# Edge counts in four groups with centred fields, row statistics on ScalarE, and a reordered graph stage

## The chip, the core and the metric

One NeuronCore of a Trainium2 chip runs the whole program. The metric is the device time of one execution in microseconds. The engines are TensorE (PE; its weight loads are PEld), VectorE (DVE), ScalarE (ACT), GpSimd (POOL) and SyncE (SP), which issues most DMAs. Each runs its own list of instructions in order; they wait for each other by semaphores.

## What is computed

625 nodes with 768 features pass through two layers, each a graph part and a mixture of experts. The change touches only the first layer's graph convolution, its attention, and the norm ahead of its experts:

```python
z = layernorm(x)                                   # 625 x 768, over the features
row, col = src, dst, each with n loops added       # 20625 edges in src, dst
dinv = rsqrt(segment_sum(1, col))                  # degrees
x = x + segment_sum((z @ W)[row] * (dinv[row] * dinv[col])[:, None], col) + b
u = layernorm(x)
xn = rmsnorm(u) * norm1_w                          # queries = keys = values, 12 heads of 64
ao = softmax(xn_h @ xn_h.T / sqrt(64)) @ xn_h      # for each head h
xf = rmsnorm(u + ao) * norm3_w                     # goes to the router, the shared and the routed experts
x = x + u + ao + moe(xf)
```

The second layer (attention over edges, then experts of width 1536) reads the same matrix of edge counts.

## The kernel before

**Edge counts.** The edges become a 625 x 625 matrix of counts CT: 165 chunks of 125 edges. For each chunk VectorE writes a one-hot of the sources (L1396, 628 columns) and one of the targets (L1397, 314 columns), in two-byte floats; the targets' 625 columns are folded to 314 by giving the upper half the weight 4096 (`FIELD`). TensorE multiplies them (L2042, L2045: 4 x 314 + 2 x 157 columns) into PSUM. A ring of five chunks (`EU`) lies between. One PSUM sum holds lower + 4096 x upper count, so the chunks are cut into six groups (`GROUPS`), which alternate between two halves of PSUM. After each group the sum is unpacked: ScalarE rounds out the upper part (`upper_counts`, L1047 to L1051), VectorE subtracts it (`lower_counts`, L1404, L1406) and adds both parts to CT (L1417, L1427). A constant row of 1 and -66 (`SHIFT`) keeps the lower part centred. VectorE does this between the next group's one-hots, along with the row statistics of x (L1366), their mean and root, and the norm (L1378). TensorE transposes the first half of the normed rows late in the last group.

**Node products and sums over edges.** All float32 products are made of two-byte pairs: high x high, low x high, high x low. Once the counts are done, ScalarE splits off their high part CTh (L1067), VectorE the low part CTl (L1473). TensorE makes h in five tiles of 125 rows (`node_products`, 36 matmuls each, L2073), the degrees as 50 matmuls of CTh and CTl with a column of ones (L2097), and transposes the counts for a mask and for layer 2 (`counts_turned`, float32, L2083). ScalarE scales h by the root into hth (L1039), VectorE makes the rest htl (L1487). The sum over edges (L2120, L2124) runs tile by tile; the self loop is a product with the identity (L2122).

**Norm of the tiles.** For each tile VectorE adds the sum to the rows (`summed`, L1503), takes their statistics (L1509, L1513) and asks ScalarE for two roots (L1080). It refines them in four small steps between the next tile's work, and ends with two scalars (L1561, L1562). ScalarE then writes the tile's 12 heads twice (L1083, L1085) and the normed row z (L1087), VectorE their low part (`heads_low`, L1527). The next root stands behind these on ScalarE.

**Heads.** For 12 heads and five tiles: TensorE transposes the heads (`sides_transposed`, L2138), makes scores (L2153, L2155), VectorE their maximum (L1579), ScalarE the exponential (L1104). TensorE transposes the weights (L2172), VectorE copies them (L1588), ScalarE makes the high part (L1113), GpSimd the low part (L961). TensorE makes the weighted sum one head behind (L2186), ScalarE takes it out (`sum_out`, L1120), TensorE turns it back (`sum_back`, L2194), VectorE divides (`fin`, L1601), GpSimd adds it to z (`head_joined`, L968). Then all engines meet (`fence`), ScalarE squares z (L1026), VectorE multiplies z by the norm's weight (L1782), the root is taken, and ScalarE scales the rows (L1168) for the shared expert.

The order is written out by hand for each engine. The program prints the functions that the diff touches:

## Time and profile before

| | us |
|---|---|
| median of 3 runs | 1620.09 (1619.05 to 1623.38) |
| profiled execution | 1621.49 |
| its span | 1619.9 |
| edge counts | to 137.8 |
| sums over edges begin | 189.1 |
| first exponential of the heads | 230.8 |
| first scaled row ahead of the experts | 393.5 |
| TensorE busy in the span | 1474.3 (91%) |
| VectorE, ScalarE, GpSimd busy | 1263.2, 873.3, 332.4 |

The span runs from the first to the last instruction; the profiled execution's own time is 1.6 us longer. A row of a timeline gives start, duration and the instruction, and in brackets how long its engine had been idle and for whom. Durations of neighbours on one engine overlap a little, so a rhythm is read from starts.

### The profile page before, as it was taken

Reading aid. Unit: us, or ns where it says so; the run is one execution under the profiler, and the core shown is the slowest. Engines: PE = TensorE matmul, PEld = TensorE weight load, DVE = VectorE, ACT = ScalarE, POOL = GpSimd, SP = SyncE. Lnnn points to the kernel's source line nnn. Section 1 sums busy time; section 2 is a strip of 40 time slices with the busy share of each in tenths; the row PEclk is TensorE's granted clock in tenths of the full one; section 3 lists DMA queues with packets and bytes.
Section 4 is the critical chain, followed back from the end, with each engine's and each line's share of the span. In section 5 each row is a group of like instructions: output and inputs, shape, how many; then the busy total and the mean of one; then the engine's idle time right before and its main releaser. Section 6 shows DMA issues by size and latency. Waiting matters only on the chain.

```text
span 1619.9 us, 36985 instructions
## 1 busy us (share of the span) xinstructions
PE 1474.3 (91%) x14673; PEld 1271.2 (78%) x14673; DVE 1263.2 (78%) x2191; ACT 873.3 (54%) x1235; POOL 332.4 (21%) x254
## 2 busy tenths in 40 slices
PE   7988968885999999999999889866999999999996
PEld 5666756664767899999998644445999999999994
DVE  8998477774565688888888679867988888888785
ACT  1113257776344567776775135554666665666651
POOL 0000416562040000000004047753600000000050
PEclk9999979997999999999999779977999999999999
DMA  7640000002475788888886011126888888888883
GB/s 203 157 121 1 11 0 1 1 1 98 138 231 174 253 276 300 302 297 296 305 286 197 1 32 32 33 88 214 280 311 285 301 285 296 302 290 295 294 267 96
DMA packets 55557, 297.61 MB, mean 184 GB/s; under 512 B 14064, under 2 KB 14320, under 8 KB 32434
## 3 DMA queue, kind: packets, MB, share of 16 engines
q1 hardware_dynamic: 41761, 263.23, 47.9%
q0 software_dynamic: 13712, 33.26, 7.6%
q8 instruction: 54, 0.88, 0.2%
q14 instruction: 30, 0.24, 0.0%
HBM read 264.07 MB, written 32.34 MB: 183 GB/s over the span
## 4 chain that ended last, share of the span: by engine, by line
PE 69%; DVE 19%; ACT 4%; issue 3%; POOL 2%; DMA 2%; SPq 0%; POOLq 0%; DVEq 0%; ACTq 0%
PE ps L744 14%; PE ps L723 9%; PE ps L725 9%; PE ps L727 9%; PE ps L2274 5%; PE ps L2257 5%; DVE wl L1396 3%; DVE wl L1397 3%; PE ps L2386 2%; POOL wl L996 2%; DMA ext<-in_units 2%; PE ps L2186 2%; DVE wl L600 2%; PE ps L756 1%; PE ps L2172 1%
## 5 line engine op out<-in xcount | busy, mean ns | idle before, releaser
L723 PE MATMUL ps<-big,wh 128*128 128x176 f16 x2160 | 496.3, 240 | 9.0 <-DVE wl L600 5.2
L727 PE MATMUL ps<-big,wl 128*128 128x176 f16 x2160 | 496.4, 238 | 0.0
L725 PE MATMUL ps<-big,wh 128*128 128x176 f16 x2160 | 496.3, 238 | 0.0
L744 PE MATMUL ps<-big,wh 128*128 128x176 f16 x2160 | 262.7, 238 | 3.8 <-DVE big L634 3.8
L744 PE MATMUL ps<-big,wl 128*128 128x176 f16 x1080 | 248.9, 239 | 0.0
L600 DVE SCALAR_TENSOR_TENSOR wl<-ext,wh 128x2304 f16<-128x2304 f32 x90 | 229.7, 2552 | 1.5 <-issue 0.9
L600 DVE SCALAR_TENSOR_TENSOR wl<-raw,wh 128x2304 f16<-128x2304 f32 x90 | 229.5, 2550 | 0.0
L519 ACT ACTIVATE wh<-raw 128x2304 f16<-128x2304 f32 x90 | 190.4, 2117 | 57.5 <-PE ps L744 53.7
L723 PEld LDWEIGHTS ps<-big,wh 128*128 128x128 f16 x2160 | 208.7, 97 | 12.8 <-issue 4.3
L519 ACT ACTIVATE wh<-ext 128x2304 f16<-128x2304 f32 x90 | 190.5, 2117 | 51.2 <-PE ps L744 35.6
L725 PEld LDWEIGHTS ps<-big,wh 128*128 128x128 f16 x2160 | 211.2, 98 | 0.2
L727 PEld LDWEIGHTS ps<-big,wl 128*128 128x128 f16 x2160 | 208.2, 96 | 0.0
L744 PEld LDWEIGHTS ps<-big,wh 128*128 128x128 f16 x2160 | 188.3, 97 | 5.3 <-DVE big L634 4.8
L2042 PE MATMUL ps<-wl 126*128 126x314 f16 x660 | 113.9, 300 | 19.5 <-DVE wl L1397 19.4
L744 PEld LDWEIGHTS ps<-big,wl 128*128 128x128 f16 x1080 | 104.4, 97 | 0.0
L961 POOL TENSOR_TENSOR ext<-raw,ext 125x625 f16<-125x625 f32 x60 | 80.3, 1339 | 103.0 <-ACT ext L1113 102.5
L486 POOL DMA_DIRECT2D y_slots<-big x16 | 11.7, 733 | 420.0 <-ACT big L549 420.0
L996 POOL TENSOR_TENSOR wl<-wl,logs 125x625 f32<-125x625 f32 x60 | 83.2, 1414 | 68.8 <-DVE wl L1935 68.8
L630 DVE TENSOR_TENSOR big<-ps,ext 128x176 f32<-128x176 f32 x108 | 36.6, 339 | 67.3 <-ACT ext L542 65.2
L2042 PEld LDWEIGHTS ps<-wl 126*128 126x128 f16 x660 | 59.7, 99 | 35.6 <-DVE wl L1397 14.7
L2386 PE MATMUL ps<-raw,wh 125*65 125x512 f32 x240 | 80.7, 481 | 6.1 <-ACT raw L1243 6.1
L480 POOL DMA_DIRECT2D big<-x_slots x17 | 12.7, 745 | 343.3 <-PE ps L707 304.7
(363 smaller groups left out, 2814.5 us busy)
## 6 DMA issues: line engine op xcount, KB each, us to landing
raw<-in_units SPq DMA_DIRECT2D x54, 1152.0 KB
ext<-in_units SPq DMA_DIRECT2D x54, 1152.0 KB
raw<-in_units SPq DMA_DIRECT2D x36, 1153.0 KB, 5.9
ext<-in_units SPq DMA_DIRECT2D x36, 1153.0 KB, 6.4
raw<-in_units_s SPq DMA_DIRECT2D x16, 769.0 KB, 4.6
ext<-in_units_s SPq DMA_DIRECT2D x16, 769.0 KB, 4.5
x_slots<-raw SPq DMA_DIRECT2D x1, 8976.0 KB
big<-x_slots POOLq DMA_DIRECT2D x17, 528.0 KB, 8.6
```

The costliest lines, as they stand in the source:

```text
L519: nc.scalar.activation(wh[:, u % RING, 0:ph.wide], raw[u % RING][:, 0:ph.wide], ACT.Copy, scale=WS).then_inc(ph.hi, 1)
L600: nc.vector.scalar_tensor_tensor(out=wl[:, u % RING, 0:ph.wide], in0=raw[u % RING][:, 0:ph.wide], scalar=WS, in1=wh[:, u % RING, 0:ph.wide ...
L723: nc.tensor.matmul(o, wh[:, u % RING, w_], x_, start=c == 0 and m == 0, stop=False, skip_group_check=True)
L725: nc.tensor.matmul(o, wh[:, u % RING, w_], xTl[:, c, 0:ph.n], start=False, stop=False, skip_group_check=True)
L727: ins = nc.tensor.matmul(o, wl[:, u % RING, w_], x_, start=False, stop=c == KC - 1, skip_group_check=True)
L744: ins = nc.tensor.matmul(o, l_[:, u % RING, w_], r_, start=first and k == 0 and c % 2 == 0, stop=last and k == 2, skip_group_check=True)
L961: nc.gpsimd.tensor_tensor(pT[:, 1, h % 2, :, own], key_blocks(n), pT[:, 0, h % 2, :, own], ALU.subtract).then_inc(s_wlo, 1)
L996: nc.gpsimd.tensor_tensor(power[:, (h * NT + t) % 4, :], power[:, (h * NT + t) % 4, :], logs[:, t, :], ALU.add).then_inc(s_masked, 1)
L2042: nc.tensor.matmul(ps[:, at + i * BANK:at + i * BANK + TH], hot[0:k, s, i * P:i * P + 128], hot[0:k, s, TP:TP + TH], start=first, stop=las ...
L2257: ins = nc.tensor.matmul(shared_up(j)[:, 0:n], l_[:, j % RING, w_], r_[:, c, t0 * P:t1 * P], start=c == 0 and k == 0, stop=c == KC - 1 and ...
L2274: ins = nc.tensor.matmul(shared_sum(t)[:, n0:n1], l_[:, j % 2, own], r_[:, j % RING, D + n0:D + n1], start=fresh and k == 0, stop=last and ...
L2386: ins = nc.tensor.matmul(sumsT[:, n0:n1], values[:, t, h, :], prob[:, t, n0:n1], start=t == 0, stop=t == NT - 1)
```

## The change

- The counts are made in four groups of 9, 8, 8 and 8 (times five chunks). The field is 5792, the constant row carries 50 and -7276 (`CENTRE`) so that both parts are centred, and `MIDDLE` is added back when unpacking. ScalarE rounds after scaling by 1/5792.
- The sources' one-hot is 626 columns wide; the two columns that were spare hold ones for all edges, so that the last row of CT's wider view CTD (127 partitions) is the degrees. Five float32 transposes (`degree_rows`) bring them to the partitions; the 50 matmuls go.
- The row statistics and the norm of x move from VectorE to ScalarE, ahead of its first unpacking: a sum, a sum of squares of the centred rows, a root, five scaled rows.
- On ScalarE the degrees' root stands ahead of the split of the counts. On VectorE the degrees and two bias rows come first, then the root, then three bias rows and the low counts.
- The self loop is no product any more: VectorE adds dinv^2 x h to the rows (second instruction of `node_low`). The counts are transposed from two-byte CTh, into two PSUM banks in turn.
- In the norm of the tiles the next root is asked before the last small step and is taken on ScalarE ahead of this tile's heads. Of tile 4 only head 0 is written before the heads begin; the other eleven and row z follow once the first sides are out.
- The squares of z are taken in four parts (`PARTS`): heads 0 to 3 during head 6, 4 to 7 during head 10, 8 to 10 behind the last exponential, head 11 after the fence. z times the weight likewise runs in two parts ahead of the fence, and head 11 is added to z by VectorE straight from PSUM.
- At the end ScalarE takes head 10's sum out ahead of the last high weights.

```diff
-GROUPS = ((0, 6), (6, 12), (12, 18), (18, 23), (23, 28), (28, 33))
+GROUPS = ((0, 9), (9, 17), (17, 25), (25, 33))
 TP, TH, TQ = 628, 314, 157
-FIELD = 4096.0
-SHIFT = 66.0
-ROUND = 1.5 * 2.0 ** 35
+PD, ROWS = P + 2, 626
+FIELD = 5792
+CENTRE = (50, 7276)
+ROUND = 1.5 * 2.0 ** 23
+MIDDLE = tuple(divmod(CENTRE[0] * CENTRE[1] * EU * (j1 - j0), FIELD) for j0, j1 in GROUPS)
...
+PARTS = (0, 4 * HD, 8 * HD, 11 * HD, D)
...
+            def squares(g, t):
+
+                own = slice(PARTS[g], PARTS[g + 1])
+                nc.scalar.activation(junk[t][:, own], z[:, t, own], ACT.Square,
+                                     accum_out=st[:, t, g, 0:1]).then_inc(s_part, 1)
...
+            act.wait_ge(s_x, 32)
+            for t in range(NT):
+                nc.scalar.activation(z[:, t, :], xres[:, t, :], ACT.Identity,
+                                     accum_out=st[:, t, 0, 0:1]).then_inc(s_part, 1)
+            act.wait_ge(s_part, NT)
+            nc.scalar.activation(st[:, :, 1, 0], st[:, :, 0, 0], ACT.Copy, scale=-1.0 / D).then_inc(s_part, 1)
+            act.wait_ge(s_part, NT + 1)
+            for t in range(NT):
+                nc.scalar.activation(z[:, t, :], xres[:, t, :], ACT.Square, bias=st[:, t, 1, 0:1],
+                                     accum_out=st[:, t, 2, 0:1]).then_inc(s_part, 1)
+            root()
+            count["sq"] += 1
+            act.wait_ge(s_var, count["sq"])
+            for t in range(NT):
+                nc.scalar.activation(z[:, t, :], xres[:, t, :], ACT.Identity, bias=rs[:, 2, t:t + 1],
+                                     scale=rs[:, 3, t:t + 1]).then_inc(s_rowsok, 1)
             upper_counts(0)
-            root()
...
-            act.wait_ge(s_unp, 3 * len(GROUPS))
+            root()
             nc.scalar.activation(CTh, CT, ACT.Copy).then_inc(s_nh, 1)
-            root()
...
+            both_roots(0)
+            for t in range(NT):
+                if t + 1 < NT:
+                    both_roots(t + 1)
                 count["sq"] += 1
                 act.wait_ge(s_var, count["sq"])
-                nc.scalar.activation(vst[t][:, :, 0, :], all_heads(t), ACT.Copy,
-                                     scale=pair[:, 2, t, 1:2]).then_inc(s_vh, 1)
-                nc.scalar.activation(vst[t][:, :, 2, :], all_heads(t), ACT.Copy,
-                                     scale=pair[:, 2, t, 1:2]).then_inc(s_vh, 1)
-                nc.scalar.activation(z[:, t, :], xres[:, t, :], ACT.Identity, bias=pair[:, 2, t, 0:1],
-                                     scale=pair[:, 3, t, 0:1])
+                if t + 1 < NT:
+                    heads_high(t, 0, H)
+                    row_out(t)
+            heads_high(NT - 1, 0, 1)
...
+            heads_high(NT - 1, 1, H)
+            row_out(NT - 1)
...
+                if h in (6, 10):
+                    if t == 0:
+                        act.wait_ge(s_madd, h - 2)
+                    squares((h - 6) // 4, t)
+            sum_out(H - 2)
             weight_high(H * NT - 1)
-            sum_out(H - 2)
+            act.wait_ge(s_madd, H - 1)
+            for t in range(NT):
+                squares(2, t)
...
-                nc.vector.tensor_scalar(hot[0:P, s, 0:TP], iota16[:, :], edges_f[:, 0, c:c + 1], None, ALU.is_equal)
+                nc.vector.tensor_scalar(hot[0:P, s, 0:ROWS], iota16[:, 0:ROWS], edges_f[:, 0, c:c + 1], None, ALU.is_equal)
...
+            dve.wait_ge(s_deg, 1)
+            nc.vector.tensor_scalar(rs[:, 0, :], degree_rows()[:, :, PD - 1], 1.0, None, ALU.add).then_inc(s_var, 1)
+            dve.wait_ge(s_vec[0], 16)
+            dve.wait_ge(s_vec[1], 16)
+            for t in range(2):
+                nc.vector.tensor_tensor(xres[:, t, :], xres[:, t, :], vec[:, 0, :], ALU.add)
+            root_of(dinv[:, :])
+            step(nc.vector.tensor_scalar(rs[:, 3, :], dinv[:, :], 1.0 / WS, None, ALU.mult))
+            step(nc.vector.tensor_tensor(rs[:, 2, :], rs[:, 3, :], dinv[:, :], ALU.mult))
+            nc.vector.memset(dot[0:1, 0:1], 0.0).then_inc(s_var, 1)
+            for t in range(2, NT):
+                ins = nc.vector.tensor_tensor(xres[:, t, :], xres[:, t, :], vec[:, 0, :], ALU.add)
...
+                nc.vector.scalar_tensor_tensor(out=xres[:, t, :], in0=node_sum(t), scalar=rs[:, 2, t:t + 1],
+                                               in1=xres[:, t, :], op0=ALU.mult, op1=ALU.add).then_inc(s_aggv, 1)
...
+            node_low(0)
+            node_low(1)
+            masked_counts(0)
+            masked_counts(1)
+            node_low(2)
+            masked_counts(2)
+            masked_counts(3)
+            node_low(3)
+            masked_counts(4)
+            node_low(4)
...
+                if more_:
+                    both_roots_asked(t + 1)
                 step(nc.vector.tensor_tensor(inv, inv, tmp, ALU.mult))
...
-                    both_roots_asked(t + 1)
-                heads_low(t)
+                    row_weighted_1(t + 1)
+                    dve.wait_ge(s_vh, 2 * t + 1)
+                    heads_low(t, 0, H)
+            dve.wait_ge(s_vh, 2 * NT - 1)
+            heads_low(NT - 1, 0, 1)
...
+            dve.wait_ge(s_vec[0], 32)
+            dve.wait_ge(s_madd, H - 1)
+            row_weighted(0, PARTS[3])
+            dve.wait_ge(s_mback, H)
+            for t in range(NT):
+                ins = nc.vector.scalar_tensor_tensor(
+                    out=z[:, t, PARTS[3]:D], in0=bank(7)[0:P, 128 + t * HD:128 + (t + 1) * HD],
+                    scalar=cols[:, 4 + (H - 1) % 2, t:t + 1], in1=z[:, t, PARTS[3]:D], op0=ALU.mult, op1=ALU.add)
+            ins.then_inc(s_madd, 1)
+            dve.wait_ge(s_madd, H)
+            step(row_weighted(PARTS[3], D))
...
+            for n0, n1 in ((0, BANK), (BANK, D)):
+                node_products(0, n0, n1)
+            node_products(1, 0, BANK)
+            pe.wait_ge(s_unp, 3 * len(GROUPS))
+            for i in range(NT):
+                ins = nc.tensor.transpose(degree_rows()[:, i, 0:PD], CTD[:, NT - 1, i * P:(i + 1) * P],
+                                          ident[0:PD, 0:PD])
+            ins.then_inc(s_deg, 1)
+            node_products(1, BANK, D)
+            for t in range(2, NT):
+                if t >= 3:
+                    pe.wait_ge(s_aggv, t - 2)
                 node_products(t, 0, BANK)
+                if t == 2:
+                    pe.wait_ge(s_var, 3)
+                    pe.wait_ge(s_nh, NH_CT + 1)
+                counts_turned(2 * t - 4)
                 node_products(t, BANK, D)
+                if t < 4:
+                    counts_turned(2 * t - 3)
...
-                        nc.tensor.matmul(o, ident16[0:P, 0:P], r_[:, i, n0:n1], start=False, stop=False)
```

The order of TensorE after the last edge chunk, before (from the 256-column half of row tile 0 on; `raw` and `big` hold W's high part and the rows, `wl` the split counts, L2097 are the degrees, L2083 transposed counts):

```order
L2073 MATMUL ps<-raw,big 125x256 x18
L2073 MATMUL ps<-raw,big 125x512 x18
L2073 MATMUL ps<-raw,big 125x256 x18
L2097 MATMUL ps<-iota,wl 125x1 [waits s_node_low]
L2097 MATMUL ps<-iota,wl 125x1 x49
L2083 MATMUL ps<-ident,big 125x125 [waits s_var]
L2083 MATMUL ps<-ident,big 125x125 x4
L2073 MATMUL ps<-raw,big 125x512 x18
L2073 MATMUL ps<-raw,big 125x256 x18
L2083 MATMUL ps<-ident,big 125x125 [waits s_cdv]
L2083 MATMUL ps<-ident,big 125x125 x4
L2073 MATMUL ps<-raw,big 125x512 [waits s_node_low]
```

And after (L2153 are the node matmuls, L2175 the degrees, L2163 transposed counts):

```order
L2153 MATMUL ps<-raw,big 125x256 x18
L2153 MATMUL ps<-raw,big 125x512 x18
L2175 MATMUL ps<-ident,big 125x127 [waits s_unp]
L2175 MATMUL ps<-ident,big 125x127 x4
L2153 MATMUL ps<-raw,big 125x256 x18
L2153 MATMUL ps<-raw,big 125x512 x18
L2163 MATMUL ps<-ident,wl 125x125 [waits s_node_high,s_var]
L2163 MATMUL ps<-ident,wl 125x125 x4
L2153 MATMUL ps<-raw,big 125x256 x18
L2163 MATMUL ps<-ident,wl 125x125 x5
L2153 MATMUL ps<-raw,big 125x512 [waits s_aggv]
L2153 MATMUL ps<-raw,big 125x512 x17
```

The degrees stand ahead of tile 1's second half, need only CT itself, and are five transposes; tile 3 waits for VectorE's self term (`s_aggv`) and no longer for the low part of h.

VectorE at the same place, before (L1359 ends the gate's split, L1473 makes the low counts, L1477 adds the bias rows, L1479 reads the degrees, L1487 the low part of h, L1493 a mask):

```order
L1359 SCALAR_TENSOR_TENSOR g<-gates,g 128x6x8 [waits s_v]
L1473 TENSOR_TENSOR wl<-big,wl 125x3125 [waits s_node_high,s_v]
L1477 TENSOR_TENSOR xres<-xres,vec 125x768 [waits s_vec1,s_vec0]
L1477 TENSOR_TENSOR xres<-xres,vec 125x768 x4
L1479 TENSOR_SCALAR rs<-ps 125x5 [waits s_deg]
L1330 RECIPROCAL dinv<-rs 125x5 [waits s_sq]
L1331 TENSOR_TENSOR rs<-dinv 125x5 [waits s_v]
L1332 TENSOR_TENSOR rs<-rs 125x5 [waits s_v]
```

And after (L1518 degrees, L1522 and L1528 bias rows, L1530 low counts):

```order
L1518 TENSOR_SCALAR rs<-ps 125x5 [waits s_deg,s_v]
L1522 TENSOR_TENSOR xres<-xres,vec 125x768 [waits s_vec1,s_vec0]
L1522 TENSOR_TENSOR xres<-xres,vec 125x768
...
L1526 MEMSET dot 1x1 [waits s_v]
L1528 TENSOR_TENSOR xres<-xres,vec 125x768 x3
L1530 TENSOR_TENSOR wl<-big,wl 125x3125 [waits s_node_high]
L1536 SCALAR_TENSOR_TENSOR xf<-ps,rs,xf 125x768 [waits s_node_high,s_v]
L1538 SCALAR_TENSOR_TENSOR xres<-ps,rs,xres 125x768
L1536 SCALAR_TENSOR_TENSOR xf<-ps,rs,xf 125x768 [waits s_node_high]
L1538 SCALAR_TENSOR_TENSOR xres<-ps,rs,xres 125x768
```

The low counts have moved behind degrees, root and bias rows, and each low part of h is followed by the self term.

ScalarE in the norm of the tiles, before (L1080 roots, L1083 and L1085 heads, L1087 row z):

```order
L1080 ACT_TABLE_LOAD [waits s_var]
L1080 ACTIVATE pair<-pair 125x2 [waits s_logs]
L1083 ACTIVATE wh<-ext,pair 125x12x64 [waits s_var]
L1085 ACTIVATE wh<-ext,pair 125x12x64
L1087 ACTIVATE z<-xres,pair 125x768
L1080 ACTIVATE pair<-pair 125x2 [waits s_var]
L1083 ACTIVATE wh<-ext,pair 125x12x64 [waits s_var]
```

And after (L1107 roots, L1112 heads, L1117 row z):

```order
L1107 ACT_TABLE_LOAD [waits s_var]
L1107 ACTIVATE pair<-pair 125x2 [waits s_logs]
L1107 ACTIVATE pair<-pair 125x2 [waits s_var]
L1112 ACTIVATE wh<-ext,pair 125x12x64 [waits s_var]
L1112 ACTIVATE wh<-ext,pair 125x12x64
L1117 ACTIVATE z<-xres,pair 125x768
L1107 ACTIVATE pair<-pair 125x2 [waits s_var]
L1112 ACTIVATE wh<-ext,pair 125x12x64 [waits s_var]
```

The roots of tile t + 1 stand ahead of the heads of tile t.

## Rows read from the trace of the kernel before

**Rows 1.** Windows, all engines: stretch, length, busy us (x instructions), PEclk, DMA share, GB/s.

```profile
10.00:50.00 40.00, 37.94 (x320) 28.75 (x319) 38.62 (x123) 5.83 (x6) 0.00 (x0) 1.00 0.73 204
...
222.00:226.00 4.00, 0.29 (x1) 0.10 (x1) 2.01 (x9) 2.72 (x5) 0.00 (x0) 0.50 0.00 0
260.00:280.00 20.00, 18.32 (x144) 13.48 (x140) 14.75 (x30) 14.58 (x29) 12.74 (x10) 1.00 0.00 1
```

**Rows 2.** Waits of 0 to 140 us: us in total, times, longest.

```profile
PE ps L2042 <- DVE wl L1397: 19.4, 15, 7.9
```

**Rows 3.** Timeline, VectorE: start, duration, instruction.

```profile
60.76 0.37 DVE L1396 TENSOR_SCALAR wl<-iota,edges_f 125x628 f16<-125x628 f16 x1
...
63.02 0.37 DVE L1396 TENSOR_SCALAR wl<-iota,edges_f 125x628 f16<-125x628 f16 x1
```

**Rows 4.** Timeline, TensorE, edge chunks.

```profile
9.15 1.25 PE L2042 MATMUL ps<-wl 126*128 126x314 f16 x4
...
50.20 0.71 PE L2042 MATMUL ps<-wl 126*128 126x314 f16 x4
...
57.61 0.69 PE L2042 MATMUL ps<-wl 126*128 126x314 f16 x4
```

**Rows 5.** Groups by line of 0 to 330 us: busy, mean ns | idle before.

```profile
L1396 DVE TENSOR_SCALAR wl<-iota,edges_f 125x628 f16<-125x628 f16 x165 | 61.6, 373 | 1.5 <-PE ps L2045 1.1
...
L1404 DVE SCALAR_TENSOR_TENSOR wl<-wh,ps 125x1256 f32<-125x1256 f32 x6 | 8.7, 1452 | 2.3 <-ACT wh L1051 2.3
...
L1417 DVE TENSOR_TENSOR big<-big,wh 125x1560 f32<-125x1560 f32 x5 | 8.9, 1771 | 0.0
...
L1366 DVE BATCH_NORM_STATS2 st<-xres 125x6 f32<-125x384 f32 x10 | 5.0, 542 | 0.0
...
L1378 DVE TENSOR_SCALAR z<-xres,mv,rs 125x768 f32<-125x768 f32 x5 | 3.3, 663 | 0.0
```

**Rows 6.** Timeline, graph stage: ScalarE, VectorE, then TensorE.

```profile
137.84 1.22 ACT L1047 ACTIVATE wh<-ps 125x1256 f32<-125x1256 f32 x1 [5.58 <-PE ps L2045]
...
156.63 3.42 DVE L1473 TENSOR_TENSOR wl<-big,wl 125x3125 f16<-125x3125 f32 x1 [1.83 <-ACT wl L1067]
...
150.22 8.25 PE L2073 MATMUL ps<-raw,big 128*125 128x512 f16 x55 [0.44 <-DVE raw L1461]
160.10 3.17 PE L2097 MATMUL ps<-iota,wl 125*125 125x1 f16 x50 [1.63 <-DVE wl L1473]
...
165.72 7.99 PE L2073 MATMUL ps<-raw,big 128*125 128x512 f16 x36
...
174.09 6.02 PE L2073 MATMUL ps<-raw,big 128*125 128x512 f16 x36
...
189.10 1.29 PE L2120 MATMUL ps<-xf,wl 125*125 125x512 f16 x5 [1.50 <-DVE xf L1487]
```

**Rows 7.** Timeline, tiles' norm and first head: VectorE, TensorE, ScalarE.

```profile
206.15 0.17 DVE L1541 RECIPROCAL pair<-pair 125x2 f32<-125x2 f32 x1 [0.81 <-ACT pair L1080]
...
211.96 0.17 DVE L1541 RECIPROCAL pair<-pair 125x2 f32<-125x2 f32 x1 [0.82 <-ACT pair L1080]
...
222.82 0.29 PE L2138 MATMUL ps<-ident,wh 125*128 125x125 f16 x1 [5.58 <-DVE wh L1527]
...
228.51 1.28 ACT L1104 ACT_TABLE_LOAD   x1
230.80 0.78 ACT L1104 ACTIVATE raw<-ps,cols 125x625 f32<-125x625 f32 x1 [1.01 <-DVE cols L1579]
```

**Rows 8.** Timeline, end of the heads: TensorE, then ScalarE.

```profile
378.31 3.76 PE L2186 MATMUL ps<-ext,wh 125*128 125x512 f16 x16 [0.63 <-issue]
...
386.53 0.84 ACT L1026 ACTIVATE big<-z 125x768 f32<-125x768 f32 x1 [3.19 <-DVE rs L1346]
...
390.79 1.28 ACT L1019 ACT_TABLE_LOAD   x1
...
393.46 1.76 ACT L1168 ACTIVATE xf<-xf,rs 125x768 f32<-125x768 f32 x2 [1.17 <-DVE dot L1785]
```

183 lines of the change are left out of this document (79 added, 104 removed).

## The prediction

> **What bounds the kernel now.** I read the page's slices and the chain first, then the windows, the waits, the groups by line and the timelines of the four places that the diff touches. All lie before 395 us of a span of 1619.9 us; behind them the diff only renames, so everything later should move as a block. Up to about 137 us the edge counts run. VectorE is busy 38.62 of 40 us there and TensorE 37.94 [rows 1], which looks like a tie; but TensorE stood still 15 times for a one-hot, 19.4 us in all, 7.9 of them at the start: 11.5 us belong to VectorE [rows 2]. In the attention heads all engines take turns and TensorE is the fullest (18.32 of 20 us) [rows 1].
>
> **Edge counts.** One chunk costs VectorE (63.02 - 60.76) / 4 = 0.565 us [rows 3] and TensorE (57.61 - 50.20) / 11 = 0.674 us, once its clock is up [rows 4]. So TensorE is the slower of the two, and only VectorE's other work makes it wait. Removed from VectorE: ten half-row statistics (10 x 0.542 = 5.4 us), five norms (5 x 0.663 = 3.3), about 0.6 of means, and two of five unpackings inside the loop, each 1.452 + 0.39 for the low part and two additions of 1.771, less overlap 5.14 us, so 10.3 [rows 5]. Together 19.6. Left on VectorE from 7.3 us on: 165 x 0.565 = 93.2, a first unpacking of 4.0, two of 5.14, a root of 1.3: end 116. TensorE's floor is the new bound: start at 8.1, four chunks at the low clock (1.31 us each, from the four matmuls of 1.25 against 0.71 later [rows 4]), 161 x 0.674 = 108.5, 15 transposes between of 1.75: 123.6. To this come waits. The ring holds five chunks. An unpacking gives pauses of 1.76, 1.69 and 1.69 us, five chunks apart, and five chunks win back only 5 x 0.109 = 0.55; a full ring (3.4 us less the handing over) is empty at the third pause, about 1 us short. Following both engines chunk by chunk with these numbers I get 137.9 for the present kernel (the trace has 137.84 [rows 6]) and 126.6 for the new one, 3.0 of it waits. **-11.2 us**; bounds: -14.3 with no wait at all, -8 if the waits double.
>
> ScalarE's new work there is hidden. Five rows summed and five squared at 0.84 us (the duration of a square of 768 columns [rows 8]), two table loads of 1.28, five norms of 0.92. x is on chip somewhere between 11 and 17.7 us, so the squares end at 22 to 28; VectorE asks for the root only after 35 chunks, at about 31. The norms end near 40.3, and group 0 (45 chunks now) at 40.9: ScalarE is free 0.6 us before it must unpack. If it is late, the unpacking slips behind ring slack; price at most 1 us.
>
> The one-hot row shrinks from 628 to 626 columns, which is no multiple of four. L1396 takes 373 ns for 628 columns [rows 5]; a slower element rate would hit 165 instructions. The Trainium skill (Vector Engine (DVE) Microarchitecture Reference, section 5.1) says that the four-element rate needs two-byte operands and an even or matching outermost count, and that an uneven last tick only drops its missing element; by that rule nothing changes. No row of this case shows 626 columns; the rival below prices it.
>
> **Graph stage**, counted from E, the end of the counts (137.8 now). Unchanged up to E+17, where VectorE has finished the low weights, both additions and the gates. Now: TensorE runs until 158.5 (55 matmuls from 150.22), VectorE splits the counts (3.42 us, from 156.63), and 50 one-column matmuls for the degrees take 3.17 [rows 6]; that slow patch also costs the clock: behind it the 36 matmuls of row tile 2 take 7.99 us against 6.02 for tile 3 [rows 6]. New: after 54 of the 72 node matmuls, E+18.4, five transposes of 0.14 us bring the degrees at E+19.1. VectorE adds two bias rows (1.8), takes the root (1.0) and two factors: E+22.6. ScalarE, which now does the root ahead of the split, ends the high counts at E+22.5 and the first two high node tiles at E+24.4. VectorE is late next: three bias rows (2.7), low counts (3.4), then low tile and self term, 0.95 each. The first self term ends at E+30.6; TensorE has finished tiles 0 to 2 and two transposed counts by E+27.6 and waits 3.0 us for that PSUM bank. Tiles 3 and 4 take 5.8 each plus 0.4 per transposed count: E+43.5. High part, low part 2.0: the sums over edges start at E+45.6, against 189.10 = E+51.3 [rows 6]. **-5.7 us.**
>
> Then 20 identity matmuls go, 2 x (0.215 + 0.110) us per tile; TensorE needs 4.9 instead of 5.5 per tile (0.65 less). The rhythm now is 211.96 - 206.15 = 5.81 us [rows 7] and belongs to a loop: ScalarE does the heads and the row before the next root, so VectorE stands 0.8 us at the reciprocal. With the root asked and taken ahead of the heads, VectorE's own work is left: 4.93 us from reciprocal to the end of the low heads, plus 0.14 for the high heads, 5.07. Walked through: first sum out E+50.5; second tile E+55.4; then 60.5, 65.6, 70.6; last root E+76.5; one head of tile 4 and not twelve: transposes ready E+78.0, sides out E+78.9. Now the sides are out at 228.5 = E+90.7, where the table load before the first exponential begins [rows 7]. From the start of the sums that is 33.3 against 39.4: **-6.1 us.** The eleven heads and the row left over (0.85 + 0.85 + 0.92) now stand on ScalarE between the sides and the first exponential, with its table load behind them: E+82.75 against 230.80 = E+93.0 [rows 7]: **+1.5 us** given back. Bounds of these three together: -14 to -5.
>
> TensorE's clock: in the wait of 3.0 us it may fall. In the present kernel it fell within a gap of 5.58 us that ended at 222.82 [rows 7]: it stands at 0.50 in 222 to 226 us [rows 1]. The new gap is little over half of that one, and matmuls fill the time before it. I take no fall; a fall costs what tile 2 shows, 7.99 - 6.02 = 2.0 us, plus 0.6 of transposes. The Trainium skill (TensorE: Matmul & The Clock Gate, "Part 4: PE-mode transpose") says transposes do not count as activity of the array as matmuls do; the five ahead of the gap would then lengthen it, and the sum be 2.6 us worse. The trace's slow patch behind one-column matmuls is akin but does not decide it.
>
> **Heads.** Ten squares of 256 columns join ScalarE in heads 6 and 10. A square of 768 takes 0.84 [rows 8]; by columns plus the fixed part 0.42 each. ScalarE is busy 14.58 of 20 us [rows 1]; four of five squares fall in its idle, the one at tile 4 delays an exponential that TensorE takes up at once, by 0.34. **+0.7 us**, bounds 0 and 10 x 0.42 = 4.2.
>
> **End of the heads.** The last weighted sum starts at 378.31 [rows 8], waiting for head 10's sum and the low weights on GpSimd. ScalarE now takes head 10 out 1.5 us sooner, then GpSimd (two tiles until 377.3) ends last: -0.9. Behind the last sum_back at 384.7 now stand a join on GpSimd (0.9), squares from 386.53 (5 x 0.84), a table load at 390.79, the root and the first scaled row at 393.46 [rows 8]: 8.8 us. New: five small PSUM additions 0.8, five 64-column products 0.7, fence 0.2, five squares of 64 columns 1.6, table load 1.28, root 1.3: 5.9. The product over 704 columns and squares of 192 run beside the last weighted sum. 0.9 + 2.9 = **-3.7 us** rounded; bounds -6 (the slow clock there, 16 matmuls in 3.76 us, gone too) and -2.
>
> **Sum.** -11.2 - 5.7 - 6.1 + 1.5 + 0.7 - 3.7 = -24.5. The profiled execution took 1621.49 us (1.6 around its span), so 1597.0; the median of the runs is 1.4 lower: 1595.6, told as 1596.
>
> **Rivals.**
> (a) The clock falls in the new wait and VectorE's waits are dearer: edge -8, graph stage 2.6 worse, squares 2 worse: 1603.6. For it: every one of these stretches hands over between engines, and I let nearly all latencies vanish. 0.16.
> (b) Deeper gain: the gap before the heads shrinks from 5.6 us [rows 7] to under 4 and the heads start at full clock. Now the first ten microseconds of heads run at half clock; five tiles with scores and transposes slower by about 0.8 each, so 4 us, and 1.6 at the tail: 1590. Against: I count 4.9 us of gap. 0.10.
> (c) Shown no gain in the edge stage: the change does not do what it says, because ScalarE's statistics come late (x late) or TensorE's ring waits stay 11.5 us; then only the later parts count, -13.3: 1607. Against it rows 2 to 4. 0.05.
> (d) The slower side: the 626-column one-hot loses its element rate. Half rate adds 628 x 0.26 = 0.163 us per chunk; VectorE at 0.73 then bounds the stage, E = 145, which still leaves 1614. At a quarter of the rate it adds 0.49: VectorE needs 165 x 1.055 = 174 plus 16, E = 197, and the total is 1621 + 59 - 13 = 1667. It decides from 0.21 us more per one-hot: the counts may end at 126.6 + 24.5 = 151 before all is lost, and VectorE ends at 116 + 165 x 0.21. Against: 314 columns, also no multiple of four, cost 0.275 from issue to issue. 0.03.
>
> **How the numbers follow.** Forecast 0.66, (a) 0.16, (b) 0.10, (c) 0.05, (d) 0.03. The forecast's own range is 1591 to 1601. To hold 8 in 10 I take in (b) and (a) and stop short of (c): 1588 to 1605. What a measurement of this kernel can tell from no change is 0.3%, 4.9 us. Only (d) ends slower: faster 0.96, same 0.01, slower 0.03.
>
> **What would show it.** Counts end near 126.6 us; TensorE's waits for one-hots fall from 19.4 to about 11; edge sums start 45.6 us behind that; rhythm of the tiles 5.1; first exponential near 209; a stand of TensorE near 3 us before tile 3, clock at 1.00 after it; first scaled row 5.9 us behind the last sum_back. Wrong if the one-hot's duration moves from 373 ns, if VectorE waits for ScalarE's roots in the loop, or if an exponential in heads 6 and 10 is late at every tile.

## The result, and the profile after

The changed kernel took 1604.58 us (median of 4 executions, 1600.18 to 1608.05), beside 1621.37 us for the kernel before on the same chip: a ratio of 0.9892, 95% interval [0.9872, 0.9912], so 17 us less, a gain 7 to 8 us smaller than forecast. Another set of five executions, made during the experiments, gave 1598.63 (1598.10 to 1601.08) beside 1620.75: 0.9859 [0.9836, 0.9882], a gain of 22. So the gain is 17 to 22 us, depending on the set. The predicted 25 lies outside the interval of the first (14 to 21) and inside that of the second (19 to 27).

The profiled execution took 1604.37 us (span 1602.6). In the windows (columns as in [rows 1]) TensorE is now the fuller engine in the counts, 40.00 of 40 us against VectorE's 37.70, and its clock falls behind the counts and at row tile 3, where in the kernel before it fell only behind the one-column matmuls (tile 2 of [rows 6]); at the start of the heads it is low as before (0.53; 0.55 in 219 to 237 us of the kernel before):

```profile
10.00:50.00 40.00, 40.00 (x342) 31.04 (x341) 37.70 (x121) 19.68 (x32) 0.00 (x0) 1.00 0.73 202
126.00:142.00 16.00, 11.51 (x46) 7.14 (x45) 11.89 (x15) 5.92 (x8) 0.00 (x0) 0.68 0.00 0
158.00:166.00 8.00, 6.15 (x26) 3.78 (x27) 6.32 (x9) 0.72 (x1) 7.04 (x1) 0.79 0.00 0
204.00:222.00 18.00, 8.93 (x39) 6.30 (x39) 10.67 (x31) 11.43 (x19) 1.29 (x1) 0.53 0.00 0
```

The waits of 0 to 130 us. TensorE's waits for one-hots fell from 19.4 us in 15 times [rows 2] to

```profile
PE ps L2122 <- DVE wl L1452: 10.9, 6, 8.1
```

as forecast (about 11). ScalarE shows a wait that the prediction does not have at all:

```profile
ACT raw L1088 <- DMA y_slots<-raw: 19.4, 1, 19.4
```

The one-hot's groups (45 to 115 us; busy, mean ns | idle before): 626 columns take 380 ns, against 373 for 628 in [rows 5].

```profile
L1451 DVE TENSOR_SCALAR wl<-iota,edges_f 125x626 f16<-125x626 f16 x95 | 36.1, 380 | 0.4
```

The graph stage (start, duration, instruction), ScalarE, VectorE, then TensorE, answers to [rows 6]:

```profile
120.77 4.51 ACT L1088 ACTIVATE raw<-ext 128x768 f16<-128x768 f32 x6 [19.43 <-DMA y_slots<-raw]
125.18 1.83 ACT L1044 ACTIVATE big<-ps 128x625 f16<-128x625 f32 x3
127.38 1.22 ACT L1058 ACTIVATE wh<-ps 127x1256 f32<-127x1256 f32 x1 [0.36 <-PE ps L2125]
...
127.05 2.25 DVE L1400 TENSOR_TENSOR big<-ps,big 128x625 f16<-128x625 f32 x3 [2.38 <-ACT big L1044]
...
129.35 2.94 PE L2113 MATMUL ps<-ident,z 125*128 125x125 f32 x15 [2.01 <-DVE big L1400]
134.28 6.99 PE L2153 MATMUL ps<-raw,big 128*125 128x512 f16 x17 [1.99 <-issue]
...
147.83 0.71 PE L2175 MATMUL ps<-ident,big 127*125 127x127 f32 x5
...
159.85 5.79 PE L2153 MATMUL ps<-raw,big 128*125 128x512 f16 x18 [2.91 <-DVE xres L1538]
...
168.01 4.05 PE L2153 MATMUL ps<-raw,big 128*125 128x512 f16 x18
...
176.41 3.30 PE L2198 MATMUL ps<-xf,wl 125*125 125x512 f16 x10 [2.09 <-DVE xf L1536]
179.51 2.02 PE L2201 MATMUL ps<-xf,wl 125*125 125x512 f16 x5
```

ScalarE begins the high split of the node weights (L1088) only when the zero fill of y_slots has landed, at 120.77. So the high rows of the first half (L1044) end at 127.0; VectorE's low rows (L1400) and the second transposes on TensorE (L2113) come late, and these transposes start 2.0 us behind the counts, run at half clock (2.94 us; 1.82 in e11_after_again at full clock), and so do the first node matmuls (17 in 6.99 us). Row tile 3, behind its wait of 2.91 us, takes 5.79 us for 18 matmuls where tile 4 takes 4.05. The degrees' transposes (L2175) start 20.4 us behind the counts and not 18.4 as forecast, and the first sums over edges are slow again.

The tiles' norm and the first head (VectorE, TensorE, ScalarE) answer to [rows 7]: the rhythm of the reciprocals is 5.02 us, not 5.81, and none of them waits (the first tile's, at 187.37, still did: 0.68). TensorE still stands 4.79 us for the last but one tile's heads. The first exponential starts at 215.54, not 230.80.

```profile
203.09 0.16 DVE L1602 RECIPROCAL pair<-pair 125x2 f32<-125x2 f32 x1
...
208.11 0.16 DVE L1602 RECIPROCAL pair<-pair 125x2 f32<-125x2 f32 x1
...
208.25 0.28 PE L2218 MATMUL ps<-ident,wh 125*128 125x125 f16 x1 [4.79 <-DVE wh L1587]
...
211.09 0.69 ACT L1135 ACTIVATE big<-ps 128x625 f16<-128x625 f16 x1 [1.16 <-PE ps L2218]
...
214.25 1.28 ACT L1145 ACT_TABLE_LOAD   x1
215.54 0.78 ACT L1145 ACTIVATE raw<-ps,cols 125x625 f32<-125x625 f32 x1
```

The end of the heads (TensorE, then ScalarE) answers to [rows 8]:

```profile
362.23 3.82 PE L2266 MATMUL ps<-ext,wh 125*128 125x512 f16 x16 [1.50 <-POOL ext L975]
...
366.63 0.69 ACT L1161 ACTIVATE big<-ps 128x625 f32<-128x625 f32 x1 [1.85 <-PE ps L2266]
...
374.64 1.76 ACT L1218 ACTIVATE xf<-xf,rs 125x768 f32<-125x768 f32 x2 [1.17 <-DVE dot L1865]
```

Measured between anchors in the profiled executions, in us (E is the start of the last ScalarE unpacking):

```
                            before   forecast   after   zeros from xf (e1_zero)
E                           137.84    126.6    127.38   126.66
E to sums over edges         51.26     45.6     49.03    45.40
sums to first exponential    41.70     37.15    39.13    39.12
to head 11's sum taken out  151.85    151.65   151.09   150.85
to first scaled row          10.81      7.9      8.01     8.01
first scaled row at         393.46    369.0    374.64   370.04
from there to the end      1226.44   1226.44  1227.96  1228.16
```

### The profile page after: what moved, and what is told of

Its sections match the earlier page's. It is cut to its first block, busy times and chain, and to the rows that moved or that the text cites. A ratio compares the mean times of both kernels' runs of the same rounds, so it can differ in the third digit from the quotient of the medians.

```text
span 1602.6 us, 36904 instructions
## 1 busy us (share of the span) xinstructions
PE 1472.8 (92%) x14608; PEld 1271.1 (79%) x14608; DVE 1253.8 (78%) x2181; ACT 883.2 (55%) x1287; POOL 332.0 (21%) x253
## 4 chain that ended last, share of the span: by engine, by line
PE 67%; DVE 16%; ACT 4%; POOL 4%; DMA 3%; issue 3%; another core or an unknown queue 1%; SPq 0%; DVEq 0%; ACTq 0%; POOLq 0%
PE ps L758 13%; PE ps L737 9%; PE ps L739 9%; PE ps L741 9%; PE ps L2354 5%; PE ps L2337 5%; POOL wl L1009 2%; DMA ext<-in_units 2%; DVE wl L1451 2%; PE ps L2266 2%; PE ps L2466 2%; DVE wl L1452 2%; DVE wl L614 2%; PE ps L770 1%
```

## The experiments

Three explanations stand against each other. Theory Z: what is missing in the graph stage is the zero fill. Theory K: the rest is TensorE's clock, which falls in waits that the forecast took as harmless. Rival P: the engines' own chain is late there. E stays the start of the last unpacking on ScalarE. Unless said otherwise, times inside a kernel are those of its one profiled execution.

**e1_zero**: the zeros come from another tile, and ScalarE waits for the fill only ahead of its first write to that tile, behind the counts.

```diff
-            nc.gpsimd.memset(raw01[:, 0, 0:D], 0.0).then_inc(s_const, 1)
+            nc.gpsimd.memset(xf[:, 0, :], 0.0).then_inc(s_const, 1)
-                         raw01[0:B // 2, 0:1, 0:D].to_broadcast([B // 2, 2 * NTAB + 2, D])).then_inc(s_zero, 16)
+                         xf[0:B // 2, 0:1, :].to_broadcast([B // 2, 2 * NTAB + 2, D])).then_inc(s_zero, 16)
...
-            act.wait_ge(s_zero, 48)
             act.wait_ge(s_wg, 16)
...
+            act.wait_ge(s_zero, 48)
             node_high(0)
```

> The changed kernel, but the zeros that are written to x_slots and y_slots now come from xf and not from raw01, so the high split of the node weights (which overwrites raw01) no longer waits for that fill (19.4 us of wait on ScalarE in the changed kernel, ending at 120.8 us). Theory Z (the fill is what made the graph stage start late): the weight split runs well before 120 us, VectorE goes on to the low rows at once (no 2.4 us wait behind its last one-hot), the second batch of transposes starts within 1 us of the end of the counts (2.0 before), everything behind is 2 to 3 us earlier, and if the shorter gap also keeps TensorE's clock at 1.00 there, up to 5: 1604.6 falls to 1600 (1599 to 1602.5). Rival P (VectorE's and TensorE's own chain was late anyway): at most 1 us, 1603.6 to 1605.

Measured: 1599.81 us (1596.47 to 1602.16), ratio to before 0.9856 [0.9834, 0.9879]. Timeline, ScalarE then TensorE:

```profile
100.54 4.49 ACT L1087 ACTIVATE raw<-ext 128x768 f16<-128x768 f32 x6
...
126.47 1.76 PE L2113 MATMUL ps<-ident,z 125*128 125x125 f32 x15
...
157.18 4.10 PE L2153 MATMUL ps<-raw,big 128*125 128x512 f16 x18 [2.91 <-DVE xres L1538]
...
172.06 3.77 PE L2198 MATMUL ps<-xf,wl 125*125 125x512 f16 x10 [2.09 <-DVE xf L1536]
175.63 1.54 PE L2201 MATMUL ps<-xf,wl 125*125 125x512 f16 x5
```

The weight split runs at 100.54, the second transposes follow the counts without a wait, and the sums start 45.40 us behind E: the forecast had 45.6. Theory Z holds for that execution of the changed kernel, and P falls. Of the 3.6 us, 2.0 had been lost by the start of tile 3 (E + 32.5 there, E + 30.5 here), 1.1 of them by the second transposes at half clock (2.94 us for 1.8). The other 1.7 came through the clock in tile 3 itself: behind the same wait of 2.91 us it takes 4.10 us here and not 5.79. That this second part belongs to the fill is not shown; e8_norm_order and e11_after_again speak against it.

**e2_fill_graph** keeps TensorE busy in the two waits:

```diff
+            def fill(n):
+                for _ in range(n):
+                    nc.tensor.matmul(bank(7)[0:P, 384:512], ident16[0:P, 0:P], iota16[0:P, 0:128], start=True, stop=True)
...
+                if t == 2:
+                    fill(40)
                 if t < 4:
                     counts_turned(2 * t - 3)
+            pe.wait_ge(s_cdv, 4)
+            fill(30)
             pe.wait_ge(s_nl, NL_CT + 1)
```

> As e1_zero, and TensorE runs 40 matmuls of 128 columns with no use in its wait ahead of row tile 3 of the node products, and 30 in its wait ahead of the sums over edges, so that it never stands still there. Theory K (the clock falls because TensorE stood still): granted clock 1.00 through tile 3 and through the first sums; the 18 matmuls of 512 columns of tile 3 take 4.05 us and not 5.79, the first 15 of the sums 3.6 and not 5.3; against e1_zero -3 us (-2 to -4). Rival: the filling delays what it stands ahead of, or the clock falls all the same: 0 to +1.5 against e1_zero.

Measured: 1596.32 us (1594.99 to 1604.93), 0.9841 [0.9820, 0.9863]. TensorE's timeline:

```profile
154.54 2.50 PE L2112 MATMUL ps<-iota,ident 125*125 125x128 f16 x40
...
157.90 4.10 PE L2159 MATMUL ps<-raw,big 128*125 128x512 f16 x18 [0.58 <-DVE xres L1538]
...
170.53 1.91 PE L2112 MATMUL ps<-iota,ident 125*125 125x128 f16 x30
172.78 2.34 PE L2208 MATMUL ps<-xf,wl 125*125 125x512 f16 x10 [0.34 <-DVE xf L1536]
174.97 1.24 PE L2211 MATMUL ps<-xf,wl 125*125 125x512 f16 x5
```

The first 15 matmuls of the sums take 3.4 us, against 5.1 in e1_zero (3.77 + 1.54, less their overlap), and the first exponential comes 37.36 us behind the sums' start, not 39.12: 1.8 us from the clock alone. That is the distance forecast (37.15). The filling delays nothing. Tile 3 gained nothing, since its clock had held in e1_zero too. So the expected 3 us were 1.8. The medians of the two lie 3.5 us apart, more than these anchors explain.

**e3_fill_heads** adds fill(76), fill(20) and fill(30) ahead of the sides of tiles 3 and 4 and of the third scores.

> As e2_fill_graph, and the same filling in TensorE's waits ahead of the heads: 76 matmuls ahead of the side of row tile 3, 20 ahead of tile 4, 30 ahead of the third scores. Theory K: the clock stays at 1.00 from 205 to 222 us, where it is 0.50 in the changed kernel; the first heads' scores and transposes take 0.38 and 0.77 us from the start and not 0.65 and 1.37: against e2_fill_graph -3.5 us (-2 to -5; my estimate of 4 for the start of the heads in the prediction's rival b). Rival: ScalarE (five exponentials of 0.78 and their partners) sets the pace there and TensorE's low clock is hidden: 0 to -1.

Measured: 1596.40 us (1592.33 to 1598.76), 0.9842 [0.9821, 0.9864]. Its window at the start of the heads, where the changed kernel has 0.53 (204 to 222 above):

```profile
200.00:218.00 18.00, 13.34 (x133) 10.68 (x132) 11.66 (x27) 14.17 (x25) 3.71 (x3) 1.00 0.00 1
```

The first head takes 9.95 us from exponential to exponential, against 11.65; to head 11's sum taken out it is 147.88 us against 149.53 in e2_fill_graph. So the slow clock at the start of the heads costs 1.7 us: not the 3.5 expected here, nor the 4 of rival (b). ScalarE, busy 14.17 of the 18 us, may set part of the pace there; no run separates that. The medians of e2_fill_graph and e3_fill_heads do not show the 1.7 us.

**e5_stats** puts the rows' statistics and norms back on VectorE, with the old row_stats, row_means and row_normed; four groups stay.

```diff
-                    if j == 6:
-                        row_roots_asked()
-                    if j == 7:
-                        rows_shifted()
+                    if 2 <= j <= 6:
+                        ins = row_stats(j - 2)
+                    if j == 10:
+                        row_means()
+                    if j == 12:
+                        root_of(rs[:, 3, :])
+                    if j in (16, 17, 18, 22, 23):
+                        ins = row_normed((16, 17, 18, 22, 23).index(j))
```

> The changed kernel with one part undone: the statistics, means and norms of the rows ahead of the counts are VectorE's again (ten half rows, five aggregates, five norms), four groups kept. My prediction's sum: VectorE has 9.3 us more to do; five norms come back at full, statistics at the start find TensorE at its low clock. By following the two engines: TensorE bounds the stage, so of 9.3 us some 5 come back (counts end at 132, 131 to 134), 1604.6 + 5 = 1609.5 (1608 to 1612). Rival Z: with the zero fill landing at 120.7 the stage behind the counts was late anyway, so that 2 of these 5 us cost nothing: 1607.5.

Measured: 1603.89 us (1597.65 to 1607.27), 0.9889 [0.9870, 0.9909]. ScalarE:

```profile
122.18 4.51 ACT L1073 ACTIVATE raw<-ext 128x768 f16<-128x768 f32 x6 [17.47 <-DMA y_slots<-raw]
126.59 1.83 ACT L1044 ACTIVATE big<-ps 128x625 f16<-128x625 f32 x3
130.74 1.22 ACT L1058 ACTIVATE wh<-ps 127x1256 f32<-127x1256 f32 x1 [2.32 <-PE ps L2128]
```

The time lies below both that were expected (1609.5 and 1607.5). E is 130.74, only 3.4 later than in the changed kernel, where 5 were expected. And the sums start at 176.15 against 176.41: nothing lost against that execution. The fill lands at 122.18 here, 8.6 us ahead of E, and delays nothing (the degrees' transposes start at E + 18.5, tile 3 takes 4.10 us); there the fill cost 2.0 us and the clock in tile 3 another 1.7. Against e11_after_again, the second execution of the changed kernel, where the sums start at 174.31, undoing the move costs 1.8 us.

**e6_zero_stats** is e5_stats with the zeros from xf.

> e1_zero (zeros from xf) with the rows' statistics and norms back on VectorE, as in e5_stats. Theory Z (the fill that lands at 120.7 us binds only a count stage that ends before about 130): counts end at 130.7 as in e5_stats and the sums over edges start 45.4 us behind them, at 176.1, so this is e5_stats over again (1603.9) and 4 us slower than e1_zero. With e5_stats and the changed kernel apart by nothing that makes the statistics' move worth 4 us alone and 0 as long as the fill binds. Rival: in e5_stats something else than the fill set the graph stage, and here the sums start at 174 or earlier.

Measured: 1599.97 us (1592.91 to 1606.28), 0.9876 [0.9830, 0.9922]. E 130.08, sums at 175.49, 45.41 behind it. With the counts ending there the fill binds nothing, freed or not; with both freed (e1_zero) the sums start at 172.06. So the statistics' move is worth 3.4 us where neither the fill nor the clock in tile 3 interferes. The medians (1599.97 and 1599.81) are too scattered to show it.

**e7_zero_groups6** is e1_zero with the old six groups.

```diff
-GROUPS = ((0, 9), (9, 17), (17, 25), (25, 33))
+GROUPS = ((0, 6), (6, 12), (12, 18), (18, 23), (23, 28), (28, 33))
+                    if j == 5:
+                        row_roots_asked()
                     if j == 6:
-                        row_roots_asked()
-                    if j == 7:
                         rows_shifted()
```

> e1_zero with the old six groups (the new field and all else kept; the roots of the rows' norm are asked 10 chunks earlier so that they come ahead of the first unpacking). VectorE has two more unpackings in the loop, 10.3 us of work. Theory A (the two parts of the edge term add): counts end at 126.6 + (11.2 - 4.1) = 133.7 us, the whole 7 us slower than e1_zero. Theory B (TensorE is the floor, so VectorE's last microseconds count most and the parts overlap): VectorE has 116 + 10 = 126 us of work against TensorE's 123.6 and the ring loses a microsecond at each pause: 130.5, the whole 4 us slower.

Measured: 1606.49 us (1605.70 to 1609.42), 0.9915 [0.9888, 0.9943]. The median is 6.7 above e1_zero's, near theory A's 7, but that is luck: E is 138.95, 12.3 later than in e1_zero and outside both theories (the profiled execution, 1609.42, is the slowest of the four; the others took 1605.70 to 1606.74). ScalarE, then VectorE:

```profile
32.90 4.71 ACT L1080 ACTIVATE z<-xres,rs 125x768 f32<-125x768 f32 x5 [4.17 <-DVE rs L1419]
37.50 1.20 ACT L1058 ACTIVATE wh<-ps 127x1256 f32<-127x1256 f32 x1
...
40.59 1.46 DVE L1459 SCALAR_TENSOR_TENSOR wl<-wh,ps 127x1256 f32<-127x1256 f32 x1 [4.90 <-ACT wh L1063]
```

The first unpacking now falls behind five norms on ScalarE, and VectorE stands 4.90 us for it. TensorE waits 5.28 us there. Without this collision E would be about 134, near theory A: an estimate from E and the 4.90 us, which no run tests. Taken in one order the stage gains 7.8 us by the four groups and the smaller changes of the counts (before to e6_zero_stats, with the statistics on VectorE: 137.84 - 130.08) and 3.4 by the statistics' move. In the other order, with six groups kept, the statistics' move gains nothing (138.95 against 137.84). So the parts do not simply add; the longer first group is what makes room for the second.

Tile 3 takes 5.79 us here with the zeros from xf, and the sums behind it start at full clock with no filling (10 matmuls of L2198 in 2.34 us): the first exponential then comes 37.36 us behind the sums' start, as in e2_fill_graph. So the 1.8 us found there do not come from the filling itself.

**e8_norm_order** is e1_zero with the old order of the roots.

```diff
-                if more_:
-                    both_roots_asked(t + 1)
                 step(nc.vector.tensor_tensor(inv, inv, tmp, ALU.mult))
...
                 if more_:
+                    both_roots_asked(t + 1)
                     row_weighted_1(t + 1)
...
-            both_roots(0)
             for t in range(NT):
-                if t + 1 < NT:
-                    both_roots(t + 1)
+                both_roots(t)
```

> e1_zero with the old order in the tiles' norm: VectorE asks for the next tile's roots only behind the shift of this tile, and ScalarE takes them behind the heads and the row (the shorter sums and the split of the last tile's heads stay). By the prediction's sum: the rhythm goes from 5.02 back to 5.7 or 5.8 us, over four tiles +2.9; the start of the sums to the sides out goes from 35.3 to 38.2 or more. Whole: +3 us against e1_zero. Rival: the rhythm came from the twenty identity matmuls that are gone, and the order is worth nothing: 5.02 stays, +0.

Measured: 1601.79 us (1596.08 to 1607.88), 0.9876 [0.9843, 0.9909]. VectorE's reciprocals:

```profile
197.06 0.17 DVE L1600 RECIPROCAL pair<-pair 125x2 f32<-125x2 f32 x1 [0.82 <-ACT pair L1107]
...
202.86 0.17 DVE L1600 RECIPROCAL pair<-pair 125x2 f32<-125x2 f32 x1 [0.82 <-ACT pair L1107]
```

The rhythm is 5.80 again, and the sides are out 36.15 us behind the sums' start. In e1_zero these are 34.67 with the slow start of the sums; here the sums start at full clock, as in e2_fill_graph (32.91). Like with like the order is worth 3.2 us, as expected (3); the medians differ by 2.0. What the clock does before is in TensorE's row for tile 3 of the same profile:

```profile
157.73 7.01 PE L2150 MATMUL ps<-raw,big 128*125 128x512 f16 x18 [2.91 <-DVE xres L1536]
```

7.01 us behind the same 2.91 us wait that e1_zero left at 4.10. The zeros come from xf here too, so this loss of 2.9 us came without the fill.

**e9_end_whole** is e1_zero with the old end.

```diff
-                if h in (6, 10):
-                    ...
-                    squares((h - 6) // 4, t)
...
+            head_joined(H - 1)
...
+            fin(H - 1)
...
+            dve.wait_ge(s_madd, H)
+            step(row_weighted(0, D))
             mean_squares(1e-5)
```

> e1_zero with the old end of the heads: head 11 joined by GpSimd, all products by the norm's weight and all squares (five of 768 columns) behind it, none in heads 6 and 10. By the prediction's sum: last sum taken out to first scaled row 10.8 us and not 8.0; first exponential to last sum taken out 151.85 as before the change, against 150.85: +3.7 in all. Rival: the squares in heads 6 and 10 cost what is won, and the heads get 2 us shorter without them: +1 to +2 in all.

Measured: 1603.31 us (1600.93 to 1607.33), 0.9905 [0.9875, 0.9936]. From the last sum taken out to the first scaled row it is 10.54 us against 8.01: 2.5. The last weighted sum starts 148.4 us behind the first exponential against 146.7 (0.9 of it because the sum_back ahead ran at half clock, 2.24 us for 1.30), and takes

```profile
359.31 4.29 PE L2252 MATMUL ps<-ext,wh 125*128 125x512 f16 x16 [0.63 <-issue]
```

against 2.3 to 3.8 elsewhere, the clock again. With it the way from the first exponential to the last sum taken out is 153.30 us, not the 151.85 expected. The last exponential comes 141.57 us behind the first, with and without squares in heads 6 and 10: they cost nothing.

**e10_fill_all** is e3_fill_heads with 24 more ahead of the last weighted sum and 115 behind the last sum_back.

> As e3_fill_heads, and TensorE is also kept busy at the end of the heads: 24 matmuls of 128 columns ahead of the last weighted sum (a wait of 1.5 us) and 115 behind the last sum_back, in the wait of 7.0 us for the first scaled row. Theory K: granted clock 1.00 from 356 to 390 us; the last weighted sum takes 2.3 us (3.8 in the changed kernel), the first twelve transposes of scaled rows 1.5 us and not 2.7; in the end 1 to 2 us faster than e3_fill_heads up to the shared expert, whole 1594.5 (1592 to 1597). Rival: ScalarE's scaled rows set the pace there, 0. The profile decides, since the part behind 400 us alone scatters by several microseconds from one execution to the next.

Measured: 1597.47 us (1595.63 to 1602.65), 0.9854 [0.9831, 0.9877]: no gain. The last sum takes 2.31 us, but

```profile
361.91 8.23 PE L2112 MATMUL ps<-iota,ident 125*125 125x128 f16 x115 [1.99 <-DVEq L436]
369.97 1.45 PE L2318 MATMUL ps<-ident,xf 125*128 125x125 f32 x12
```

the filling starts 2.0 us late and at half clock (0.50 in 362 to 364 us), takes 8.23 us, and holds the transposes of the scaled rows back to 369.97, some 3 us later than due (the first scaled row is at 365.88, and they start 1.1 us behind it in the changed kernel). Too long a filling becomes the wait. The question whether the clock matters there stays open.

**e11_after_again** is the changed kernel without any edit.

> The changed kernel itself once more, as a yardstick on the chip of this call. 1604.6 again (1603 to 1606). With it a second profile: if the loss of the graph stage belongs to the zero fill, the sums over edges start at 174.4 us or later again (the fill lands at 120.7, ScalarE's weight split follows, second transposes 2.0 us behind the counts' end), whatever the clock does; if it was an accident of one execution, at 172.

Measured: 1598.63 us, as told above. ScalarE, then TensorE:

```profile
120.08 4.51 ACT L1088 ACTIVATE raw<-ext 128x768 f16<-128x768 f32 x6 [18.59 <-DMA y_slots<-raw]
...
127.52 1.22 ACT L1058 ACTIVATE wh<-ps 127x1256 f32<-127x1256 f32 x1 [1.20 <-PE ps L2125]
...
128.66 1.82 PE L2113 MATMUL ps<-ident,z 125*128 125x125 f32 x15 [1.17 <-DVE big L1400]
...
146.02 0.71 PE L2175 MATMUL ps<-ident,big 127*125 127x127 f32 x5
...
158.04 5.48 PE L2153 MATMUL ps<-raw,big 128*125 128x512 f16 x18 [2.91 <-DVE xres L1538]
...
174.31 4.03 PE L2198 MATMUL ps<-xf,wl 125*125 125x512 f16 x10 [2.09 <-DVE xf L1536]
```

The fill landed 0.7 us earlier, the second transposes waited 1.17 us and not 2.01, and ran at full clock (1.82). The sums start at 174.31, 1.4 us late and not 3.6, just ahead of the 174.4 that I had set as bound. But these 1.4 us are not the fill's. The degrees' transposes start at E + 18.50 and tile 3 at E + 30.52, as in e1_zero (18.51 and 30.52), so the late second transposes cost nothing; what is missing arises in tile 3 (5.48 us for 4.10). The way from the landing is the weight split, ScalarE's high rows, VectorE's low rows, the second transposes and their high rows. Here it ends at 132.37, while VectorE is busy with the low counts until 132.49 anyway. In the first execution the landing 0.7 us later and the transposes at half clock made it 2.0 us too late. So the fill ends last in one of two executions of the changed kernel, and costs 2.0 us or nothing.

**e12_zero_again** is e1_zero once more.

> e1_zero once more, beside the changed kernel on one chip. Theory Z: 3 to 5 us faster than e11_after_again. Second profile: the sums start 45.4 us behind the end of the counts if the clock holds in the wait of 2.91 us ahead of row tile 3 (its 18 matmuls 4.1 us), 48.3 if it falls as in e8_norm_order (7.0 us).

Measured: 1597.43 us (1597.05 to 1602.00), 0.9857 [0.9833, 0.9881]; the sums start 45.40 us behind E, tile 3 takes 4.10. Against e11_after_again that is 2.1 us up to the sums by the profiles (0.7 at E, 1.4 in tile 3), but only 1.2 in the medians, where 3 to 5 were expected. With the fill costing nothing in that profile, the pair does not show theory Z again. Over both sets of each the medians are 1600.18 (9 executions) and 1598.71 (10).

The reason for this scatter lies behind the change: from the first scaled row to the end the profiles have 1221.8 (e5_stats) to 1235.5 us (e2_fill_graph) for the same instructions. Of these 13.7 us, 8 arise between 870 and 950 us, in the second layer's attention, where the granted clock differs (0.86 against 0.73 in 870 to 920 us). A gain of 2 us is shown by anchors and not by medians. On their own chip e2_fill_graph and e3_fill_heads (1596.3 and 1596.4) lie below e1_zero (1599.8); on its own chip e10_fill_all (1597.5) equals e12_zero_again (1597.4).

## Why the prediction was right, and where it was not

The forecast was 1596 and the range 1588 to 1605; the result fell within the range, but outside the likeliest case's own 1591 to 1601, at the size of rival (a), 1603.6. The second set, 1598.6, lies inside it. Rival (a) had the clock in the new wait right, but not the edge counts, which it put 3 us worse, nor the squares; and no case of the prediction has the fill. By the steps:

**Edge counts, -11.2: measured -10.5 and -11.2 (e1_zero; -10.3 in e11_after_again).** Right: TensorE as the floor, and 3.0 us of waits inside (2.8). The row of 626 columns keeps its rate. The Trainium skill (Vector Engine (DVE) Microarchitecture Reference, section 5.1) says that a tick that lacks an element only drops that element's write, and the trace agrees: 380 ns against 373. Rivals (c) and (d) are out.

**Graph stage, -5.7: measured -2.2 and -4.5 in two executions of the changed kernel, -5.9 in e1_zero.** Two steps failed. The first is the claim "Unchanged up to E+17": 2.0 us in the first execution, nothing in the second. It took times relative to E for all that stood there. But the weight split hangs on a transfer that lands at 120 to 122 us in every profile that shows it, with E anywhere from 127 to 131 us. In the kernel before, ScalarE reached the split right behind an unpacking, with no idle time (its timeline):

```profile
121.54 4.49 ACT L1062 ACTIVATE raw<-ext 128x768 f16<-128x768 f32 x6
```

The wait was satisfied and showed in no view; with E 10.5 us earlier, the same wait ended last in the first execution, and just did not in the second. I had asked of VectorE, ScalarE and TensorE what is late next, but not of the queue. Row by row the rest held: the wait ahead of tile 3 was 2.91 us (forecast 3.0), the degrees' and the self term's order was as drawn.

**Clock in that wait, "I take no fall": the second step that failed, and the length does not settle it.** Behind 2.91 or 2.92 us without filling it fell in four of nine executions: both of the changed kernel (5.79 and 5.48 us), e7_zero_groups6 (5.79) and e8_norm_order (7.01). It held (4.10) in e1_zero, e12_zero_again, e5_stats, e6_zero_stats and e9_end_whole. It cost the changed kernel 1.7 and 1.4 us, at a forecast price of 2.0. The fill does not decide it: it was in place in e5_stats, where the clock held, and out of the way in e7_zero_groups6 and e8_norm_order, where it fell. The Trainium skill (TensorE: Matmul & The Clock Gate, "HAM oscillation — how this bites in real kernels") says that waits between groups of matmuls make the gate throttle again, so that the next group starts slow. The traces agree in those four executions and not in the other five; what decides one way or the other at the same wait, no run here shows.

**Tiles' norm, -6.1 and start of heads, +1.5: together -2.6 measured, -4.6 forecast.** The rhythm was right (5.02 against 5.07), the order alone is worth 3.2 us (e8_norm_order), and the start of the heads cost +1.5 as forecast (sides out to first exponential 4.45 us, not 3.00). The missing 2.0 is the first sum at half clock behind a wait of 2.09 us that the forecast had not counted as a risk: with the sums at full clock it came to 37.36 against 37.15 (e2_fill_graph with filling, e7_zero_groups6 without).

**Squares in heads 6 and 10, +0.7: measured 0.** The exponential at the next head's start is 0.3 late and is made up within the head.

**End of heads, -3.7: measured -2.8 and -0.8.** The last weighted sum starts 146.7 us behind the first exponential and not 147.5. The forecast's own terms, 0.9 and 2.9, make 3.8 and not 3.7.

In sum 0.8 at the counts, 3.4 in the graph stage, 2.0 in the norm and 0.1 at the end, less 0.6 gained in the heads, are the 5.7 us by which the first scaled row is later than forecast. Behind it the two profiles differ by 1.5 us more for the same instructions. Up to 397 us, in the shared expert, 1.6 us arise, where the clock fell behind the 60 sixteen-column matmuls of the gates (0.59 in 392 to 396 us), as it had not before (1.00 in 411 to 415); later the difference moves up to 4.2 and back. "Everything later should move as a block" is right on average (1227.5 us over the twelve profiles behind the change, 1226.4 in the one before) and wrong by up to nine microseconds in any one execution.

What stays open: why the first set of the changed kernel stood 6 us above the second. Between the two profiles, 5.8 us apart, the fill and the clock in the graph stage account for 2 us (176.41 and 174.31), the last weighted sum for 1.5 and the part behind for 2.3. These are one profile each; that the other executions differ for the same reasons is not shown, nor why the clock falls in one and not in the other.
